# Graph stage of a decoder kernel: the power of x's variances behind the last threshold update, the blending of x behind the adjacency, the power of the sums in a later round

## The reference, cut to what matters

```python
sim = einsum('bhnd,bhmd->bnm', Q, K) / (sqrt(d) * H)          # from the context, 512 x 512 per batch
threshold = top_k(sim, int(512 * 0.3))[0][:, :, -1:]           # the 153rd largest of each row
A = sigmoid(sim) * (sim >= threshold)
A = (A + swapaxes(A, -1, -2)) * 0.5
x = x + (1 - gamma) * layernorm(x) + gamma * A                 # the graph step
xn = layernorm(x)                                              # then the router, on xn
topk_idx = top_k(softmax(xn @ w_cls.T) + bias, 8)
```

## Time and profile before

| | us |
|---|---|
| median of 3 runs | 3081.89 (3077.84 to 3084.49) |
| the profiled execution | 3076.68 |
| its span in the trace | 3074.7 |
| graph stage, from about | 675 to 1196 |
| DVE busy in the span | 1837.2 (60%) |
| ACT busy | 1242.4 (40%) |
| POOL busy | 859.5 (28%) |
| PE busy | 2470.5 (80%) |

### The profile page before, as it was taken

The page is one execution under the profiler, slowest core; times in us unless marked ns, Lnnn a source line. Parts: engine busy times, 40 slices in busy tenths (PEclk is TensorE's granted clock), DMA queues, the critical chain, the costliest instruction groups (busy, mean ns, idle before and its releaser), DMA issues. The chain is left out here.

```text
span 3074.7 us, 34907 instructions
## 1 busy us (share of the span) xinstructions
PE 2470.5 (80%) x12662; PEld 1631.8 (53%) x12662; DVE 1837.2 (60%) x2917; ACT 1242.4 (40%) x1873; POOL 859.5 (28%) x1198
## 2 busy tenths in 40 slices
PE   5898989863531334999727999999999969999999
PEld 4454545321211223999624545545555537888887
DVE  3756566528977853777556777565555534444443
ACT  2443435328745533666402334334333323333332
POOL 2222223215667755333263333001111110000000
PEclk8999999975665666999858999999999979999999
DMA  4213131226222153899676565333433324001000
GB/s 121 58 43 83 42 82 46 69 103 265 76 70 83 58 166 113 287 304 304 209 188 160 133 178 146 101 83 95 121 100 79 100 74 159 31 11 42 1 28 14
DMA packets 200952, 340.40 MB, mean 111 GB/s; under 512 B 28809, under 2 KB 60425, under 8 KB 198754
## 3 DMA queue, kind: packets, MB, share of 16 engines
q1 hardware_dynamic: 177250, 299.80, 32.3%
q0 software_dynamic: 20480, 37.87, 4.9%
q10 hardware_dynamic: 3072, 0.79, 0.1%
HBM read 182.30 MB, written 109.05 MB: 95 GB/s over the span
## 5 line engine op out<-in xcount | busy, mean ns | idle before, releaser
L670 ACT ACTIVATE at_probs<-at_ps 128x1024 f32<-128x1024 f32 (+3 forms) x256 | 221.8, 866 | 273.7 <-PE at_ps L538 271.0
L757 DVE TENSOR_REDUCE at_negmax<-at_ps 128x2 f32<-128x1024 f32 (+3 forms) x256 | 259.0, 1015 | 122.0 <-PE at_ps L523 64.3
L1367 DVE TENSOR_REDUCE a_negmax<-a_ps 128x2 f32<-128x1024 f32 x128 | 155.1, 1216 | 137.4 <-PE a_ps L1120 136.8
L1896 ACT ACTIVATE gr_act_signs<-gr_signed,gr_test 128x512 bf16<-128x512 f32 x248 | 177.2, 716 | 133.4 <-POOL gr_test L2236 103.1
L59 PE MATMUL ff_ps<-ff_xnT_hi,ff_s_hi 128*128 128x512 f32 x512 | 201.0, 393 | 5.1 <-DVE ff_xnT_lo L2767 5.1
L61 PE MATMUL ff_ps<-ff_xnT_hi,ff_s_lo 128*128 128x512 f32 x512 | 200.2, 391 | 0.0
L60 PE MATMUL ff_ps<-ff_xnT_lo,ff_s_hi 128*128 128x512 f32 x512 | 200.1, 391 | 0.0
L538 PE MATMUL at_ps<-at_qk 98*128 98x512 f32 (+3 forms) x512 | 172.7, 420 | 20.5 <-DMA at_qk<-at_mrow 11.5
L2797 DVE TENSOR_TENSOR ff_hid<-ff_hid,ff_ps 128x512 f32<-128x512 f32 x64 | 44.0, 687 | 238.8 <-ACT ff_hid L2742 238.8
L1268 ACT ACTIVATE a_probs<-a_ps 128x1024 f32<-128x1024 f32 x128 | 131.0, 1024 | 137.1 <-PE a_ps L1138 136.6
L518 PE MATMUL at_ps<-at_qk 96*128 96x512 f32 (+3 forms) x512 | 163.9, 384 | 17.7 <-DVE at_xnT_lo L818 8.0
(11 more groups left out here) (410 smaller groups left out, 6552.9 us busy)
## 6 DMA issues: line engine op xcount, KB each, us to landing
at_qk<-at_part SPq DMA_DIRECT2D x384, 128.0 KB, 2.5
first_gu<-in_L_ffn_w_gate_up_dram SPq DMA_DIRECT2D x32, 1024.0 KB, 5.5
a_qk<-a_part SPq DMA_DIRECT2D x192, 128.0 KB, 2.4
slot_rows<-gr_zeros SPq DMA_DIRECT2D x16, 1024.0 KB
first_d<-in_L_ffn_w_down_dram SPq DMA_DIRECT2D x32, 512.0 KB, 6.4
ex_rows<-slot_rows SPq DMA_DIRECT2D x32, 512.0 KB, 4.5
out_rows<-ex_y SPq DMA_DIRECT2D x32, 512.0 KB, 3.0
gr_aside_raw<-in_L_ffn_W_dram SPq DMA_DIRECT2D x48, 256.0 KB, 3.0
```

Of the source, the lines that this page charges most:

```text
L670: act.activation(probs[:, t % 2, 2 * w:2 * w + 2, lo:S], banks(("kq", g, s), lo), ACT.Exp, scale=SCALE).then_inc(free(("kq", g, s)), 1)
L757: dve.reduce_max(negmax[:, g % 2, :].rearrange("p (j t) -> p j t", t=NT)[:, 2 * w:2 * w + 2, t], banks(("qk", g, s), 0, width(g, t)), AX.X ...
L1367: dve.reduce_max(negmax[:, g % 2, :].rearrange("p (j t) -> p j t", t=NT)[:, 2 * w:2 * w + 2, t], banks(("qk", g, s)), AX.X, negate=True).t ...
L1896: act.activation(act_signs[:, j, :], src, ACT.Sign, scale=-1.0, bias=against, accum_out=total[:, i, j:j + 1]).then_inc(counted_to[j], 1)
```

## The change

Four edits: `blend_x(b)` moves from ahead of `exact_bounds` to behind `adjacency`; `rstds(b, 0)` moves from behind round 26 (24) to behind all rounds of the batch, ahead of round 0 of the next; `rstds(b - 1, 1)` moves from behind round 4 to behind round 8 in batch 1 and behind round 5 in batches 2 and 3. Nothing is added or dropped.

```diff
             def finish(b):
                 exact_bounds(b)
                 adjacency(b)
+                blend_x(b)
                 strike_out(b + 1, 0, 2)
                 if b < B - 1:
                     add_adjacency(b)
@@
             for b in range(B):
                 blend_statistics(b)
-                blend_x(b)
                 finish(b)
@@
                 for r in range(TESTS):
                     for j in range(COUNTED[b]):
                         update(b, r, j)
-                    if b and r == 4:
+                    if b and r == (8 if b == 1 else 5):
                         rstds(b - 1, 1)
-                    if r == (26 if b else 24):
-                        rstds(b, 0)
                     if b >= 2 and r in EARLY:
                         scatter(b - 2, sent, sent + EARLY[r])
                         sent += EARLY[r]
@@
                         scatter(b - 1, r - LATE, r - LATE + 1)
+                rstds(b, 0)
             scatter(B - 2, TESTS - LATE, TESTS - LATE + 12)
             rstds(B - 1, 1)
```

## The result

The changed kernel took 3046.08 us (median of 4 runs, 3043.04 to 3051.1) beside 3081.32 us for the kernel before (4 runs): ratio 0.9888, 95% interval 0.9872 to 0.9903, so 34.5 us faster. The profiled execution took 3043.04 us, its span 3041.0 (before 3076.68 and 3074.7): 33.7 less. The last scatter, which ends the graph stage, starts at 1161.10 instead of 1195.19: 34.1 less. What was won in the stage reached the end but for 0.4.

A forecast was written before the change was run, and what follows sets the result against it. Pool and DVE were taken to bound the graph stage by waiting in turn for variances and the last threshold update. Terms -1.2 - 7.1 - 11.9 - 12.5 + 1.7 = -31.0 took 3081.89 to 3051 us, range 3043 to 3058.

The forecast's parts named there:

- delay through round 8: Batch 1: the sums' later power makes DVE's normalize 8.6 late and its variances of x 8.3; bounds 0 to 10.
- Batch 0: Rounds behind round 24: removing the power and the blending beside it lets the last update start earlier, -1.2 us.
- E0: Start of L2051, DVE's first step on a batch's last update, in batch 0; numbered on for batches 1 to 3.
- Batch 1: Turn-taking removed gives 15.3, the sums' later power takes 8.3 back; DVE sets the batch's end: -7.1 us.
- Batch 2: Scatters fill Pool's wait, search 1.5 ahead; end 10.4 earlier, Pool sets it: together -11.9 us.
- Batch 3: Power and blending delay early rounds, yet 1.8 won at round 5 and 10.7 at the end: together -12.5 us.
- The end: End of the graph stage: the new power in front adds 1.2, blending beside the scatters 0.5: +1.7 us.
- The place where row and rule differ: Moved blending beside Pool: rule holds Pool 1.9, row 0.5; forecast takes the row, 3051 rather than 3054.
- Round-8 power not on the path: Rival: batch 1 gives its whole 15.3 because the sums' later power delays nothing; 3043, chance 0.08.
- Held stretch: Rival: blending and power push Pool's first updates into L2072, costing 9 us in batches 2, 3 and end; 3060, chance 0.12.
- No change: Rival: another queue sets the stage's end or the win is waited away at the next power; 3082, chance 0.04.
- Slower: Rival: normalize waits for the sums' later power in three batches, holding DVE and ScalarE; 3089 at 15 us lateness, chance 0.03.

The follow-up runs named there:

- power_only: Kernel before with x's power alone moved behind all rounds, blending and sums' power in their old places: 3061.33 us, ratio 0.9938.
- blend_only: Kernel before with the blending of x alone moved behind the adjacency, all powers in their old places: 3078.34 us, ratio 0.9991.
- sums_old: Changed kernel with all three of the sums' powers back behind round 4: 3039.54 us, ratio 0.9885.
- b1_4: Changed kernel with batch 1's power of the sums back behind round 4: 3035.84 us, ratio 0.9862; repeated on another occasion 3040.77 us, 0.9841.
- after_again: Changed kernel measured once more, unaltered, beside a kernel before of 3088.58 us: 3051.4 us, ratio 0.988.
- b1_5: Changed kernel with batch 1's power of the sums behind round 5 instead of 8: 3038.11 us, ratio 0.9877.

## Why the prediction was right, step by step

The forecast was 3051 with 3043 to 3058, by a sum of -31.0; measured -34.5 by the ratio, -33.7 in the profiled execution. The mechanism held as written: two engines taking turns, freed by moving the power and the blending; power_only, blend_only and sums_old show it part by part. One reading behind it was looser than it looked. The totals of 48.0 and 45.2 do not belong together as they stand: of Pool's 48.0 only 33.4 (15.65, 8.76 and 9.03) are for the variances of x, the rest is for those of the sums; of DVE's 45.2, 9.7 lie in batch 0, where Pool does not wait. The pair that makes the turn-taking is 33.4 and 35.5, in batches 1 to 3. The sum did not use the totals. In the bounds there is a slip: with no delay through round 8 and nothing lost at the end, the sum's own terms give -31.0 - 8.2 - 1.7 = -41, not -39. The measured time was near neither. The sizes:

**Batch 0**: -1.2 forecast, -1.3 measured from L2251 to E0 (91.86 to 90.59), -0.8 by E0 alone. The kernels that are the same there as the changed one spread from 88.8 to 91.6, so this says no more than that the term is small.

**Batch 1**: -7.1 forecast, -8.9 measured. That DVE sets E1, with Pool 3 us ahead, is what the rows above show. The term too large was the delay through round 8, 8.3 forecast; b1_4 puts it at 6.6. Most of that is the wait of `normalize` itself: 8.6 forecast, 7.35 measured. The power's start was taken at 798.19 - 764.55 = 33.64 behind E0; it was at 795.76 - 763.75 = 32.01. Of these 1.6 us about 1.1 are TensorE's: the second pair of transposes (L1772) took 1.02 instead of 1.91, and ScalarE's copy of `gr_cT`, behind which everything to round 8 is chained, came 16.18 behind E0 instead of 17.27.

```profile
774.04 1.02 PE L1772 MATMUL gr_ps<-gr_adjacent,ident 128*128 128x512 f32 x2
```

This is not of the change. Over the runs that copy comes 15.9 to 17.3 behind E0, whatever the kernel, and in after_again it came 17.31 behind: there the wait was 7.99 and the gap 102.31, 0.7 from the forecast. The forecast's -7.1 was sized to such an execution. The other half us I did not separate.

**Batch 2**: -11.9 forecast, -11.6 measured. Pool's last update of tile 0 was done at 971.04, DVE began at 971.08: Pool sets E2, as forecast.

**Batch 3**: -12.5 forecast, -13.25 measured. **The end**: +1.7 forecast, +0.4 measured. Both terms were mis-sized by the same step, that the power behind the last update delays what follows by 1.25 and the blending by 0.5 more. The timeline of Pool and DVE around E2 shows what happens:

```profile
973.18 1.31 POOL L2240 TENSOR_TENSOR gr_rstd<-gr_mv,minus_half 128x4 f32<-128x4 f32 x1
...
974.97 2.87 POOL L2222 TENSOR_SCALAR gr_offset<-gr_half 128x1 f32<-128x1 f32 x1
...
975.27 2.50 DVE L2072 SCALAR_TENSOR_TENSOR gr_adjacent<-gr_adjacent,first_gu 128x512 f32<-128x512 f32 x4
...
978.22 2.01 DVE L2044 TENSOR_SCALAR shared_rows<-first_d,gr_blend 128x512 f32<-128x512 f32 x4
...
978.86 1.08 POOL L2248 DMA_INDIRECT slot_rows<-shared_x,slots  x1 [0.30 <-issue]
980.25 0.97 POOL L2248 DMA_INDIRECT slot_rows<-shared_x,slots  x1 [0.30 <-issue]
```

A small update of Pool stands until DVE's L2072 ends, at 977.84, 6.76 behind E2. In the kernel before a small update three instructions further on stood the same way, 2.78 us long, and ended 6.74 behind E2:

```profile
996.30 2.78 POOL L2221 TENSOR_SCALAR gr_sign<-gr_half 128x1 f32<-128x1 f32 x1
```

So the power fell into time that Pool lost anyway; only the three instructions that it pushed past that point came after. Round 4 ended 0.67 later (987.52 - 971.08 = 16.44 against 1008.11 - 992.34 = 15.77), not 1.75. That is 1.1 better than forecast; the rest of the batch gave 0.3 of it back. At the end of the stage it is a scatter that stands there:

```profile
1077.24 1.31 POOL L2240 TENSOR_TENSOR gr_rstd<-gr_mv,minus_half 128x4 f32<-128x4 f32 x1
...
1081.17 1.50 POOL L2248 DMA_INDIRECT slot_rows<-shared_x,slots  x1 [0.30 <-issue]
1082.98 1.03 POOL L2248 DMA_INDIRECT slot_rows<-shared_x,slots  x1 [0.30 <-issue]
```

It lost 0.5 instead of the 1.5 of before, and both end 7.5 behind E3. The rows of the kernel before, the scatter and then the sums' last power, and under them that power in the changed kernel:

```profile
1114.68 2.47 POOL L2248 DMA_INDIRECT slot_rows<-shared_x,slots  x1 [0.30 <-issue]
...
1128.67 1.08 POOL L2240 TENSOR_TENSOR gr_rstd<-gr_mv,minus_half 128x4 f32<-128x4 f32 x1
```

```profile
1094.23 1.07 POOL L2240 TENSOR_TENSOR gr_rstd<-gr_mv,minus_half 128x4 f32<-128x4 f32 x1
```

The power starts 19.03 behind E3 before and 19.10 after: the 1.7 forecast for this step were 0.07, almost nothing. The 0.4 that the end is longer arose behind `normalize`, and 0.4 is what this end differs by among the versions that leave it alone (85.60 in b1_4, 85.99 in b1_5).

**The place where row and rule differ**: the row was right. Beside the 2.01 us of the blending one scatter took 1.08 (the next began as the blending ended), and at the end of the stage one took 1.03 beside 2.06 us: neither was held. In batch 2, where four small instructions of Pool ran beside it, these took 1.51 us in all where the next four took 1.11. By the rule of the Trainium skill (SBUF — State Buffer, Who interferes with whom) for a `tensor_scalar` in its two-port mode, Pool would have been held 1.9 us at each. No run shows such a hold for this shape; whether the blending ran in that mode no run shows either.

The rivals. *Round-8 power not on the path*: no, it costs 6.6 (b1_4); the 15.3 that this rival gave batch 1 is what b1_4 has, 15.5, once the power is back at round 4. *Held stretch*: the stretch was met and worked the other way, taking up the power instead of adding to it. *No change*: no part of the win was waited away. *Slower*: it needed a lateness of 12.6 beyond the forecast's, and the lateness was below the forecast's: 7.35 for 8.6 in batch 1, and 2.0 for 2.1, covered, in batch 2.

The third edit is where the experiments say more than the result: sums_old, without it, can't be told from the whole by its time. The edit wins 2.0 + 3.5 in batches 2 and 3 and loses 6.6 in batch 1. Half of it, round 5 in batches 2 and 3 alone, is b1_4.

## What to carry to other kernels

Where two engines each wait for the other once an iteration, look for an instruction that each could do later, and move both: one alone moved gave 0 and 19 us here, both gave 35. Pair the waits iteration by iteration before you trust equal totals: here a third of Pool's total belonged to another wait on the same line. Before you move a producer later, read when its consumer's queue is ready, in every iteration: the same edit was worth 2 to 3.5 us in two batches and cost 6.6 in a third, where another engine happened to stretch the rounds. And price an insertion by what follows it: ahead of a stall that ends with another engine's instruction, it cost little here (0.67 and 0.07 us for a power of 1.31).

## What the runs showed of the hardware that I had not expected

- The issue of an indirect DMA on Pool is also held beside L2072, DVE's operation with two inputs from SBUF: up to 2.83 us (869.56 in the changed kernel) where it alone takes 0.97. Beside the blending, one input, it took 1.03 and 1.08.
- The power of 128x4 took 1.31 instead of 1.04 us where it ran beside DVE's L2062 and L2069 (973.18, 1077.24), in every version that has it there; beside L2051 it took 1.05 (865.11).
- The place where TensorE's clock rises moves by one or two microseconds between executions with the same work ahead of it. The second pair of transposes in batch 0 took 1.02 us at a granted clock of 1.00 in the changed kernel's profile and 1.91 at 0.50 in that of before, each behind 3.5 us of the same transposes at 0.50; two matmuls of L1818 took 1.10 at 1.00 and 2.05 at 0.50 in two executions of one kernel. In a chain that waits for them that was 1.1 us and 1.7 us, of the size of some of the terms forecast here.
